# Four target masks on VectorE, the first 0/1 tile of GpSimd earlier, and the guard's product moved: a graph attention kernel on one core

## The reference

```
h    = relu(layernorm(x))                       # x: 512 x 128
msg  = h_neigh + E[adj]                         # per target and neighbour, types are adj itself
q, k, v = h Wq^T + bq, msg Wk^T + bk, msg Wv^T + bv     # 8 heads of 16
s    = q . k / 4          where adj == 0: -1e9
a    = softmax(s, over the 512 neighbours)      where adj == 0: 0
out  = x + (a . v) Wo^T + bo
```

## Time and profile before

| | before |
|---|---|
| time, median of 3 (lowest to highest) | 52.49 us (52.41 to 52.53) |
| the profiled execution's own time | 52.74 us |
| its span, first to last instruction | 50.6 us |
| mean granted clock of TensorE | 0.99 |
| busy, share of the span: TensorE / VectorE / ScalarE / GpSimd | 87% / 80% / 68% / 61% |

### The profile page before, as it was taken

One profiled execution on the slowest core, in us unless ns is written; L12 is line 12 of the kernel. 1 busy time (PEld: TensorE's weight loads), 2 busy tenths in 40 slices (PEclk: granted clock), 3 DMA queues, 4 the chain that ended last, 5 costly groups with the idle time before them and its releaser, 6 DMA issues.

```text
span 50.6 us, 844 instructions
## 1 busy us (share of the span) xinstructions
PE 44.1 (87%) x257; PEld 17.8 (35%) x260; DVE 40.3 (80%) x115; ACT 34.7 (68%) x60; POOL 31.0 (61%) x50
## 2 busy tenths in 40 slices
PE   0899879978999679899999999999999998999800
PEld 0333215824445233234344424142222023288500
DVE  2011879598489999799999999799997999989820
ACT  0380657789996978979999898897199999400000
POOL 5790001999999999547599959990999930000000
PEclk9999999999999999999999999999999999999996
DMA  0689999960099999700000000000000000000032
GB/s 0 76 219 431 435 379 235 403 269 2 10 212 193 184 295 201 154 2 0 0 0 0 0 6 0 13 0 0 0 0 0 0 0 0 13 0 0 0 118 89
DMA packets 2070, 4.98 MB, mean 98 GB/s; under 512 B 258, under 2 KB 658, under 8 KB 1810
## 3 DMA queue, kind: packets, MB, share of 16 engines
q1 hardware_dynamic: 1490, 2.44, 21.2%
q10 hardware_dynamic: 576, 2.49, 12.7%
HBM read 3.08 MB, written 0.26 MB: 66 GB/s over the span
## 4 chain that ended last, share of the span: by engine, by line
PE 62%; DVE 15%; DMA 8%; ACT 5%; issue 3%; DVEq 0%
PE ps L609 15%; PE ps L577 11%; DMA xt<-x_dram 8%; PE ps L623 8%; PE ps L563 7%; PE ps L633 6%; PE ps L586 4%; PE ps L604 3%; PE ps L547 2%; PE ps L512 2%; DVE ctxT L476 2%; DVE stats L368 2%; DVE split L396 2%; DVE y L489 2%; DVE turned_U L467 2%
## 5 line engine op out<-in xcount | busy, mean ns | idle before, releaser
L426 DVE CUSTOM_DVE_ANT_0 masked_scores<-ps,mask_b 128x512 bf16<-128x512 f32 x32 | 20.1, 687 | 1.7 <-PE ps L563 1.0
L233 POOL TENSOR_TENSOR prob<-prob,live 128x512 int32<-128x512 int32 x10 | 12.6, 1275 | 0.0
L351 ACT ACTIVATE prob<-ps 128x512 f32<-128x512 f32 x21 | 11.4, 598 | 1.1 <-PE ps L609 0.8
L609 PE MATMUL ps<-stack 98*128 98x512 bf16 x32 | 10.9, 381 | 0.6 <-ACT stack L323 0.4
L577 PE MATMUL ps<-stack 96*128 96x512 bf16 x28 | 9.6, 384 | 0.2
L215 POOL TENSOR_SCALAR mask_b<-adj_b_sb 128x512 bf16<-128x512 int32 x3 | 6.3, 2111 | 4.8 <-DMA adj_b_sb<-adj_b_dram 4.8
L351 ACT ACTIVATE prob<-masked_n 128x512 f32<-128x512 f32 x11 | 6.4, 626 | 1.5 <-DVE masked_n L446 1.4
L446 DVE TENSOR_TENSOR masked_n<-ps,veto 128x512 f32<-128x512 f32 x11 | 6.8, 683 | 0.4 <-PE ps L609 0.3
L503 PE MATMUL ps<-ones 128*128 128x512 bf16 x10 | 4.2, 604 | 1.4 <-DVE ones L361 1.4
L323 ACT ACTIVATE stack<-ps 2x512 bf16<-2x512 f32 x8 | 4.7, 590 | 0.4
L609 PEld LDWEIGHTS ps<-stack 98*128 98x128 bf16 x32 | 2.8, 97 | 6.0 <-DVE masked_n L446 2.2
(11 more groups left out here) (71 smaller groups left out, 54.8 us busy)
## 6 DMA issues: line engine op xcount, KB each, us to landing
stack<-split SPq DMA_DIRECT2D x8, 192.0 KB, 4.0
adj_b_sb<-adj_b_dram ACTq DMA_DIRECT2D x1, 1024.0 KB, 7.4
adj_n_sb<-adj_n_dram ACTq DMA_DIRECT2D x1, 1024.0 KB, 10.1
pk<-pack_k_dram ACTq DMA_DIRECT2D x1, 322.0 KB, 4.4
xt<-x_dram SPq DMA_DIRECT2D x1, 256.0 KB, 4.2
pw<-pack_w_dram SPq DMA_DIRECT2D x1, 256.0 KB, 6.0
out_dram<-y SPq DMA_DIRECT2D x1, 192.0 KB, 2.0
brow<-bias_rows_dram SPq DMA_DIRECT2D x1, 128.0 KB, 9.1
```

The costliest lines, as they stand in the source:

```text
L233: nc.gpsimd.tensor_tensor(bits, bits, live[:, LIVE_TILES.index(t), :], ALU.mult).then_inc(cut_done, 1)
L351: nc.scalar.activation(prob[:, h, t, :], scores, ACT.Exp, scale=DH ** -0.5).then_inc(exp_done, 1)
L426: nc.vector.tensor_tensor_reduce(out=masked_scores[:, k % len(A_BANKS), :], in0=ps[:, A_BANKS[k % len(A_BANKS)], :], in1=mask_b[:, t, :], ...
L609: nc.tensor.matmul(bank, stack[0:STACK, h, SIDE["k"], t * P:(t + 1) * P], stack[0:STACK, h, SIDE["q"], :], start=(h, t) not in ON_PE, stop ...
```

## The change

GpSimd makes no target mask any more; its first work after the constants is the 0/1 tile of t = 3, for which it waits for `adj_n`. VectorE makes mask 0 between the copy of k's first part and the taking of q's first part, and masks 1, 2 and 3 each ahead of the maximum that uses it. The guard's product of bank 5 goes from ahead of head 0's scores to behind score k = 6, ahead of `turn_max(0)`.

```diff
-MASKS_ON_POOL, MASK_ON_DVE = (0, 1, 3), 2
...
@@ gpsimd
-            pool.wait_ge(adj_b_loaded, 16)
-            for t in MASKS_ON_POOL:
-                nc.gpsimd.tensor_scalar(mask_b[:, t, :], adj_b_sb[:, t * N:(t + 1) * N], 0.0, MASKED,
-                                        ALU.is_equal, ALU.mult).then_inc(mask_b_pool_ready, 1)
...
@@ vector
+            def make_mask_b(t):
+                dve.wait_ge(adj_b_loaded, 16)
+                nc.vector.tensor_scalar(mask_b[:, t, :], adj_b_sb[:, t * N:(t + 1) * N], 0.0, MASKED,
+                                        ALU.is_equal, ALU.mult).then_inc(mask_b_ready, 1)
...
             copy_slots("k", 0, k_copied)
+            make_mask_b(0)
             take_q_part(0)
...
                 if h == 0:
-                    if t in MASKS_ON_POOL:
-                        dve.wait_ge(mask_b_pool_ready, MASKS_ON_POOL.index(t) + 1)
-                    else:
-                        dve.wait_ge(mask_b_ready, 1)
+                    dve.wait_ge(mask_b_ready, t + 1)
...
             for t in range(BT):
-                if t == MASK_ON_DVE:
+                if t >= 1:
                     make_mask_b(t)
                 find_max(0, t)
...
@@ tensor
-            add_tiny(ACC_BANK, B)
             for t in range(BT):
                 score_head_0(t)
...
             for k in range(BT, 9):
                 score_by_target(k // BT, k % BT)
                 if k == 6:
+                    add_tiny(ACC_BANK, B)
                     turn_max(0)
```

More of the change, by code:

```diff
@@ L153, in gnn_kernel @@
         v_projected, v_ready, v_biased = sem("v_projected"), sem("v_ready"), sem("v_biased")
-        (mask_b_ready, mask_b_pool_ready, squares_ready, veto_even_ready, veto_odd_ready, veto_last_ready,
+        (mask_b_ready, squares_ready, veto_even_ready, veto_odd_ready, veto_last_ready,
          veto_bias_set) = (
-            sem("mask_b_ready"), sem("mask_b_pool_ready"), sem("squares_ready"), sem("veto_even_ready"),
+            sem("mask_b_ready"), sem("squares_ready"), sem("veto_even_ready"),
             sem("veto_odd_ready"), sem("veto_last_ready"), sem("veto_bias_set"))
@@ L429, in find_max @@
                     accum_out=row_max[:, h, t:t + 1]).then_inc(max_found, 1)
[L431 to L434, removed]
             adj_tiles = adj_n_sb[:, :].rearrange("p (t b) -> p t b", b=B)
```

## The result

| | before | after |
|---|---|---|
| median (lowest to highest), 20 runs each, taken together | 52.53 us (52.04 to 52.98) | 52.27 us (51.76 to 52.63) |
| ratio of after to before, 95% interval | | 0.9942 (0.9916 to 0.9968) |
| profiled execution / its span | 52.74 / 50.6 us | 52.48 / 50.5 us |

The kernel became faster by 0.58%, that is 0.30 us (0.17 to 0.44). I had forecast 52.32 us, a gain of 0.17.

What follows compares the result with a forecast made beforehand. No engine was taken to bound throughout: an engine relay until about 19 us, then TensorE and VectorE nearly full. Terms -0.11 - 0.13 + 0.07 = -0.17 us took the median from 52.49 to 52.32 us, range 52.17 to 52.70.

Steps and rivals of the forecast that it cites:

- Mask 0: On VectorE behind the k copy: its 0.46 us fits a 0.54 us gap, costing nothing, 0.08 to spare.
- The q copy: VectorE's copy, no longer held by GpSimd's first mask, takes 0.42 instead of 0.75; 0.13 us gained on the path.
- The guard: Leaving its place ahead of head 0's scores brings the first maximum 0.32 us earlier; behind k = 6 it costs 0.22, idle.
- Three masks between the maxima: On VectorE, four maxima and masks 1 to 3 take 3.84 us; fifth maximum at 16.88 against 16.55.
- The hold of mask 1: On VectorE, mask 1 is held by the end of GpSimd's first 0/1 tile: 0.07 us lost, bounds 0 and 0.29.
- rival 3: Mask 1 is held longer, as the 0/1 tile starts later or takes 2.16: loss 0.29, 52.54 us; chance 0.15.
- The sum at 18.80: Start of the first scores by neighbour: -0.11 guard and masks, -0.13 q copy, +0.07 mask 1, together -0.17 us.
- The gate: Score k = 8, awaiting the sixth maximum, decides the first score by neighbour: 18.67 to 18.70, 0.11 us gained against 18.80.
- rival 2: VectorE's last k copy is held until the 0/1 tile ends: 0.9 us slower, 53.4 us; chance 0.06.
- rival 1: The q copy is slow for itself, so only the guard's 0.11 us gain is left: 52.38 us; chance 0.16.
- Rival 4: First adjacency lands over 0.4 us later than 8.63, so mask 0 pushes q's parts: 52.6 us; chance 0.05.
- Rival 5: The start of 18.80 moves but later waits (cuts, vetoes, second turning) give it back: 52.49 us; chance 0.16.

Runs made afterwards that it cites:

- masks_only: The kernel after with the guard's product back ahead of head 0's scores; ratio to before 1.0032 (0.9999 to 1.0065).
- guard_only: The kernel before with only the guard's product moved behind score k = 6, masks as before; ratio to before 0.9897 (0.9849 to 0.9945).
- tiles_later: The kernel after with both GpSimd 0/1 tiles put behind head 0's splitting; ratio to before 0.9908 (0.9873 to 0.9942).
- guard_k5: The kernel after with the guard's product behind score k = 5 instead of k = 6; ratio to before 0.9953 (0.9908 to 0.9998).
- after_again: The kernel after, unchanged, timed and profiled again; ratio to before 0.9944 (0.9910 to 0.9977).
- tile_after_copies: The kernel after with GpSimd's first 0/1 tile also waiting for VectorE's last k copy; ratio to before 0.9871 (0.9801 to 0.9940).

## Why the prediction was right

**Mask 0** was costed at nothing, with 0.08 us to spare. It ran from 9.08 to 9.50 and q's part started at 9.54. The first adjacency was never late in a profile here.

**The q copy** was costed at 0.13 us gained. It took 0.42, and L389 behind it started at 10.88, where the forecast had 10.90. masks_only has this alone: its first maximum, at 13.60, is 13.60 - 8.78 = 4.82 behind the projection instead of 4.95, so 0.13.

**The guard** was the term with the wrong size, in both its places. Leaving gave 0.52 us at the first maximum (guard_only), not 0.32. Part of it is visible: from the last taking-away to the first score were 12.08 - 11.55 = 0.53 us before and are 11.54 - 11.42 = 0.12 now, so 0.41; the rest is VectorE's start, 1.28 us behind the first score before and 1.17 now. The eight f32 products behind the guard took 3.70 us in before and masks_only, and 3.60 without it ahead of them. In its new place it costs 0.32, not 0.22 (17.24 to 17.56), and not all of that lies in idle time: GpSimd's parts, subtracted from 17.21, would have let the turning start at 17.21 + 0.25 = 17.46.

**Three masks between the maxima** were costed at 0.46 each, and 0.61 to 0.62 for each maximum, 3.84 us in all. In tiles_later, without a hold, they take 16.43 - 12.59 = 3.84. In the kernel after they take 16.78 - 12.71 = 4.07, 0.23 for the hold.

**The hold of mask 1** was taken as 0.07 between bounds of 0 and 0.29. It was 0.23 in the profile after and 0.09 in the second one. The mechanism and the bounds were right; that it would vary from execution to execution I had only as rival 3. Two of my own signs were missed in the profile after: the first maximum was to start at 12.9 to 13.05 and came at 12.71, and mask 1 over 0.6 was to mean that the prediction is wrong: it took 0.66. Both have one cause. The first maximum came earlier than forecast, so mask 1 was wanted at 13.33 instead of 13.53, but its end hangs on the end of the tile. The second maximum then started at 14.02, where the forecast had 14.06.

**The sum at 18.80** was -0.17, a head of 10.22. The two profiles have 10.28 and 10.11. In the first, the hold took back what the guard gave beyond its 0.32, for the reason just named: that this came out near the forecast is partly luck, since the guard was mis-sized by 0.20 and the hold by 0.16.

**From the span to the time** the prediction carried 2.1 us outside the span over unchanged, without a reason. It became 1.95. So the 0.30 us measured against 0.17 forecast are not the same gain: about 0.17 of them lie in this term, and inside the span it was 0.05 to 0.13. That the time of 52.27 us came so near to 52.32 is in this part luck.

**The gate**: score k = 8, behind the sixth maximum, was named as what decides after the change. From the fifth maximum to L599 it was costed at 1.79 to 1.82 us and took 18.66 - 16.78 = 1.88: the chain of waits of guard_k5 has score k = 8 at 17.70, 0.23 behind the read-out that releases it (17.47), where I took 0.13. In the profile of after it and ScalarE's copy come nearly together: the copy ends at 17.98 + 0.59 = 18.57 and L599 starts 0.09 behind that, where it was 0.05 before. In guard_k5 the score alone decides: the copy ends at 17.34 + 0.59 = 17.93, L599 starts at 18.13.

**Rivals.** The chip refuted rival 2 (hold for a whole instruction) and rival 1 (a q copy slow for itself). Rival 2's own case, a last k copy over 0.5, did occur in two other kernels (0.57 in masks_only, 0.66 in guard_k5), by a hold at the start of the 0/1 tile, and stayed within the 0.48 us of room that the prediction gave it. Rival 3 is real but smaller. Rival 4 was not seen. Rival 5 (given back later) holds for 0.05 us at most: the rest of the path is 29.29 before and 29.34 after. In the prediction's sum for the eleventh maximum, 13.04 + 1.38 + 6.10 is 20.52 and not 20.54, which changes nothing.

**What stays open.** The times moved more than the profiles: 0.30 us (0.17 to 0.44), and much the same in after_again, against 0.06 and 0.23 on the path. The 0.17 us outside the span fill most of that distance, but what they are is not shown. Before has a single profile; its own mask on VectorE took 0.42 there and 0.87 in guard_only, so other executions of before may well have a hold which that profile lacks. This was not tried. That the two halves of the change have opposite signs inside the span rests on the timed runs' spans, with the profiles in agreement.

## What to carry to other kernels

When a change has several parts, ask which of them is the gain: here a one-row product moved by a few instructions gave all that was gained inside the span, and the large move of work between engines took much of it back there. Work that goes from GpSimd to VectorE has a second price beside its duration: it meets what is left on GpSimd, and what it loses depends on the phase, so tie GpSimd's instruction by a semaphore to the copies it must not meet instead of letting a transfer's landing decide. To find where a small change acts, take a distance inside the profile that starts behind the inputs. To find how much it is worth, take the spans and times of many runs, and look at the difference of the two: what lies outside the span can move by as much as the change.

## What the runs showed of the hardware

A GpSimd mask or 0/1 tile (128x512, int32 in, 1.94 us) held a VectorE copy or mask in SBUF that started in about its first 0.4 us (0.28 became 0.57 and 0.66, 0.42 became 0.75) or its last 0.6 us (0.42 became 0.87 and 0.66). A mask of 0.42 held at the end ended about 0.28 us behind GpSimd's end; one that started 0.06 us before the end, in tile_after_copies, took its free 0.42. In between, copies and masks ran at their free duration. A GpSimd product of two tiles held copies for 0.85 of its 1.33 us. In reverse, copies in a row on VectorE kept a GpSimd mask of 1.92 us from ending for 24.25 us.

The guard's product, one row deep, took 0.32 us of TensorE in front of another instruction at both places, where a 128-row 512-column bf16 product took 0.22.

The device time outside the span was 1.94 to 1.95 us in four of the kernels (after, masks_only, tiles_later, guard_k5) and 2.07 to 2.12 in before, with the same inputs and outputs.
